# A fourth quarter of filters loaded earlier and rounded in two places, in a recommender's interaction layers

## The reference

```
e  = stack of the 32 picked rows              # 512 x 32 x 32: sample, field h, depth d
c0 = relu(sum over h,m of e[b,h,d]*e[b,m,d] *W0[h,m,n])    # 128 maps n
c1 = relu(sum over h,m of e[b,h,d]*c0[b,m,d]*W1[h,m,n])    # 128 maps n
z  = concat(sum_d c0, sum_d c1)               # 512 x 256
y  = relu(relu([z, dense] @ W1top + b1) @ W2top + b2) @ W3top
```

## Time and profile before

| | |
|---|---|
| median of 3 runs | 844.33 us (843.94 to 844.50) |
| the profiled execution's own time | 844.57 us |
| its span, first to last instruction | 842.8 us |
| PE busy | 833.8 us, 99% |
| DVE, ACT, POOL busy | 803.8, 782.7, 726.4 us |
| granted PE clock | full in every slice |
| DMA | 60.17 MB, mean 71 GB/s |

### The profile page before, as it was taken

One profiled execution on the slowest core, in us unless ns is written; L12 is line 12 of the kernel. 1 busy time (PEld: TensorE's weight loads), 2 busy tenths in 40 slices (PEclk: granted clock), 3 DMA queues, 4 the chain that ended last, 5 costly groups with the idle time before them and its releaser, 6 DMA issues.

```text
span 842.8 us, 17221 instructions
## 1 busy us (share of the span) xinstructions
PE 833.8 (99%) x3595; PEld 670.1 (80%) x3595; DVE 803.8 (95%) x877; ACT 782.7 (93%) x2779; POOL 726.4 (86%) x550
## 2 busy tenths in 40 slices
PE   8999999999999999999999999999999999999998
PEld 6687888888888888888888888888888888888777
DVE  7689999999999999999999999999999999999996
ACT  4799999999999999999999999999999999999984
POOL 5798888999888999888899888899888799988871
PEclk9999999999999999999999999999999999999999
DMA  4551233331232332132232123332123233112000
GB/s 147 166 155 40 56 83 81 83 84 51 43 85 78 82 85 67 29 82 78 83 84 78 30 69 79 83 83 84 41 53 82 79 84 84 47 48 76 1 13 1
DMA packets 62245, 60.17 MB, mean 71 GB/s; under 512 B 26347, under 2 KB 37227, under 8 KB 62222
## 3 DMA queue, kind: packets, MB, share of 16 engines
q1 hardware_dynamic: 58126, 57.80, 23.2%
q0 software_dynamic: 4096, 2.11, 3.3%
HBM read 55.51 MB, written 4.31 MB: 71 GB/s over the span
## 4 chain that ended last, share of the span: by engine, by line
PE 94%; DVE 2%; DMA 1%; POOL 1%; issue 1%; SPq 0%; ACT 0%; DVEq 0%
PE ps_y L895 27%; PE ps_y L903 27%; PE ps_y L896 27%; PE ps_c L868 3%; PE ps_c L878 3%; PE ps_c L877 2%; PE ps_c L876 2%; POOL gat L447 1%; DVE csum L737 1%; PE ps_c L874 1%; DVE prod L724 1%; DMA prod<-w 1%; DMA gat<-table,rows 0%; PE ps_y L999 0%; POOL w_lo L454 0%
## 5 line engine op out<-in xcount | busy, mean ns | idle before, releaser
L559 ACT ACTIVATE prod<-ps_y,es 128x128 f32<-128x128 f32 x2560 | 719.6, 490 | 37.3 <-PE ps_y L903 33.2
L737 DVE TENSOR_REDUCE csum<-prod 128x64 f32<-128x1664 f32 (+2 forms) x256 | 478.8, 1871 | 0.4 <-POOL prod L436 0.2
L895 PE MATMUL ps_y<-w_hi,c_both 128*128 128x512 f32 x1024 | 415.4, 406 | 2.9 <-POOL w_lo L454 2.1
L903 PE MATMUL ps_y<-w_hi,c_both 128*128 128x512 f32 x1024 | 399.6, 390 | 0.0
L896 PE MATMUL ps_y<-w_lo,c_both 128*128 128x512 f32 x1024 | 399.4, 390 | 0.0
L724 DVE TENSOR_TENSOR prod<-ps_y,es 128x512 f32<-128x512 f32 x384 | 256.3, 681 | 23.3 <-PE ps_y L903 17.0
L436 POOL TENSOR_TENSOR prod<-prod 128x768 f32<-128x768 f32 (+1 forms) x128 | 240.4, 1878 | 36.1 <-ACT prod L559 28.1
L895 PEld LDWEIGHTS ps_y<-w_hi,c_both 128*128 128x128 f32 x1024 | 192.4, 188 | 55.3 <-issue 11.5
L896 PEld LDWEIGHTS ps_y<-w_lo,c_both 128*128 128x128 f32 x1024 | 192.4, 188 | 48.2 <-issue 8.2
L903 PEld LDWEIGHTS ps_y<-w_hi,c_both 128*128 128x128 f32 x1024 | 192.2, 188 | 41.9
L426 POOL TENSOR_TENSOR z<-first,second 128x512 f32<-128x512 f32 x155 | 198.1, 1296 | 25.0 <-PE ps_c L874 24.9
(11 more groups left out here) (119 smaller groups left out, 290.0 us busy)
## 6 DMA issues: line engine op xcount, KB each, us to landing
second<-et_scratch SPq DMA_DIRECT2D x155, 256.0 KB, 3.6
first<-et_scratch SPq DMA_DIRECT2D x31, 256.0 KB, 3.3
et_scratch<-gat SPq DMA_DIRECT2D x62, 64.0 KB
prod<-w SPq DMA_DIRECT2D x4, 512.0 KB
h_scratch<-h_sums SPq DMA_DIRECT2D x120, 2.0 KB
gat<-table,rows_now POOLq DMA_INDIRECT x116
wt_sb<-wt SPq DMA_DIRECT2D x2, 512.0 KB
rows_now<-rows SPq DMA_DIRECT2D x30, 2.0 KB, 1.8
```

The costliest lines, as they stand in the source:

```text
L559: last = nc.scalar.activation(prod[:, buffer_of(g, u), h // 2, :, h % 2], ps_y[:, bank_of(g, u, k), j * N:(j + 1) * N], ACT.Copy, scale=es ...
L737: nc.vector.tensor_reduce(csum[:, g.r, maps, u], prod[:, buffer_of(g, u), fields_folded(g, u) // 2:F // 2, maps, :].rearrange("p a n t -> ...
L895: nc.tensor.matmul(out, hi, w_hi, start=True, stop=False)
L903: nc.tensor.matmul(out, lo, w_hi, start=False, stop=True).then_inc(y_ready, 1)
```

## The change

Two things are moved. In SP's order, the last quarter of W1 is issued directly behind the second and third, before the wait for group 1's gathers, and no more after group 1's two writes. In ACT's first tile, bank 6 of W1 is rounded ahead of bank 1's scaling, followed by the wait for the other tiles' products and their `round_z` (both stood ahead of bank 3); bank 7 alone is rounded ahead of bank 3. No instruction is added or removed.

```diff
             sp.wait_ge(gathered[0], 16 * TG)
-            for n in range(1, W1_LOADS - 1):
+            for n in range(1, W1_LOADS):
                 filters(n)
...
             send(Group(0, 1))
-            filters(W1_LOADS - 1)
             fetch(Group(0, 1))
...
-                        if number == 0 and (u, k) == (0, 3):
+                        if number == 0 and (u, k) == (0, 1):
+                            round_w1((6,))
                             act.wait_ge(z_ready, KP)
                             round_z(slice(1, TG), z_hi_ready, SPLIT)
-                            round_w1((6, 7))
+                        if number == 0 and (u, k) == (0, 3):
+                            round_w1((7,))
```

## The result

The changed kernel is slower: median 846.80 us of 21 runs (845.00 to 848.16), beside 844.30 us of 21 runs of the kernel before (843.71 to 846.41). The ratio is 1.0024, with a 95% interval of 1.0018 to 1.0029, so some 2.0 us were lost where 1.7 were to be won. (The ratio takes in every run of both and lies near that of the means, 846.70 and 844.59; the medians alone are 2.5 us apart. The profiled execution took 846.53 us, with a span of 844.7 us (842.8 before). Lines of the changed kernel are shifted by one here and there: L453 is the POOL split that was L454, L762 the DVE rest that was L761, L694 `rest_z` (L693), L932 the last first-layer matmul (L931), L567 ACT's rounding (L568).

A forecast was written before the change was run, and what follows sets the result against it. PE bounds the kernel, busy 833.8 of 842.8 us. The 2.55 us stall, less 0.21 for POOL's splits behind its gathers and 0.6 for DVE's hold, gives a gain of 1.7: 842.6 us, range 841.7 to 843.3.

The forecast's parts named there:

- What bounds the kernel, and that a gain is carried to the end: PE, full from 27 to 800 us, carries an earlier start through; the start's stall is worth 2.55 us at most.
- The transfer and ACT: Last W1 quarter landed by 18.3, bank 6 rounded from 19.6; nothing on ACT comes to the path, 0.5 us to spare.
- (c): Quarters in flight share the DMA engines, so the second lands with the last: slower, 845.0 to 845.6 us; chance 0.05.
- (d): Last quarter lands behind 19.6, ACT's order blocks, or group 1's rows come late: 843.0 to 844.3 us; chance 0.07.
- SP's queue: Group 1's gathers up to 1.3 us later, read-back from 20.4 to 21.7, POOL's products 0.4 to 1.7 earlier; cost none.
- POOL's two splits: Behind POOL's last gather, they would run from 21.62 to 24.15 without a hold, a gain of 2.34 us.
- That DVE can hold POOL: A POOL instruction starting under a DVE one with two SBUF operands may be held until it is through.
- The price of the hold: At POOL's splits beside DVE's L761 and L693: none, or POOL waits for both; -0.6 us in the sum.
- rival (b): POOL gets in between DVE's two instructions, rest_z is held, PE loses 1.21 us: gain 1.3, time 843.0; chance 0.17.
- The forecast's own case: POOL's first split waits for both DVE instructions, the second ends at 24.84: gain 1.7 us, time 842.6; chance 0.35.
- 0.21 + 0.6: Deductions from the 2.55 us stall: 0.21 for POOL's two splits behind its gathers, 0.6 for the hold by DVE.

The follow-up runs named there:

- e8: Changed kernel with DVE doing the rests of banks 6 and 7, POOL none, and ACT's order as before: 842.07 us beside 844.28, ratio 0.9975.
- e4: Changed kernel with ACT's order as in the kernel before, so only SP's earlier transfer remains: 843.44 us beside 844.47, ratio 0.9983.
- e2: Changed kernel with POOL's two last filter splits waiting until DVE's bank-5 rest is done: 843.52 us beside 844.47, ratio 0.9984.
- e7: Changed kernel with POOL's last gather behind its splits, the first split waiting for DVE's scaling of bank 2: 843.13 us, a single run.
- e9: Changed kernel with a one-column memset on POOL between last gather and first split, and a wait for it: 843.04 us beside 844.42, ratio 0.9980.
- e3: Changed kernel with 11 more matmuls of zeros filling PE's wait for rest_z: 845.35 us beside 844.47, ratio 1.0004.

## Why the prediction was wrong

**What bounds the kernel, and that a gain is carried to the end:** right. PE stayed full between 50 and 800 us, and e8 carried the 2.55 us of the start to the end: 2.8 us of the span, 2.1 by the ratio (1.4 to 2.9).

**The transfer and ACT:** right. The last quarter was issued at 11.7 and took 6.1 us, so it landed at 17.8 ("by 18.3"); bank 6 was rounded at 19.69 (19.6 predicted), `round_z` ended at 20.84 (20.9 predicted), the second quarter came no later (ACT idle 0.56 us before 15.15, against 0.67): rivals (c) and (d) didn't happen.

**SP's queue:** group 1's writes went out at 18.09, 1.0 us later than before, inside the 1.3 allowed. The read-back started at 21.98, not at 20.4 to 21.7: the writes took 2.6 us after their issue, not 2.0. POOL's first product started at 26.79, 0.17 us later than before, where 0.4 to 1.7 earlier was predicted. It cost nothing: no wait of PE follows from it.

**POOL's two splits:** in the changed kernel they weren't held at all: 21.80 to 24.31, where 21.62 to 24.15 was predicted without a hold and an end at 24.84 in the forecast.

**That DVE can hold POOL:** right, and the row it was read from, the gather at 10.98, is borne out by the other profiles. In each of the fourteen, one gather starts under a DVE rest of the filters, and it is longer than 0.94 us by what that one DVE instruction still has to run, less 0.12 or 0.13 us. In e8:

```profile
9.57 0.68 DVE L754 TENSOR_TENSOR w_lo<-prod,w_hi 128x512 fp32r<-128x512 f32 x1
9.73 1.35 POOL L446 DMA_INDIRECT gat<-table,rows  x1 [0.30 <-issue]
```

0.52 us were left, and the gather took 0.40 more. In e4 0.63 were left and it took 0.50 more; in the kernel before 0.40 and 0.28. The splits of e2, e4, e7 and e9 follow the same sum: in e9 0.49 were left of `rest_z`, and the split took 0.37 more. The gather at 20.66, which spoke against it, had started before the DVE rest, not under it. The forecast let POOL wait until both DVE instructions are through; the rows show a wait for the one that runs, after which POOL's split goes ahead of the next (e7). With POOL starting as late as in e4 and e9 that one is `rest_z`, the last of the two, so the size came out by this coincidence.

**The price of the hold is the step that failed.** The mechanism was named and its ends were worked out, but for the wrong party. "Its price from both ends" ran from nothing to POOL's split waiting for DVE, and rival (b) let DVE wait for one split, from the end of the bank-5 rest: 1.21 us. The worst end, DVE waiting for both splits and from the start of the bank-5 rest on, was left out: 2.81 us. What excluded it was the assumption that an instruction already running keeps its place. e2, e4, e7 and e9 show that this holds when POOL's instruction is released after it; in the changed kernel POOL's was released at 20.34, when ACT had rounded bank 6, behind a gather that ran until 21.70. The forecast's own case is e9 and e4, with POOL's second split ending at 24.79 in e9 (24.84 predicted), and their ratios are worth 1.7 and 1.4 us, the gain that was forecast. The Trainium skill's rule (SBUF — State Buffer, on its two separate sides and on who interferes with whom: whoever starts first gets the shared pair for the whole instruction) agrees with e2, e4, e7 and e9, by the lengths above; in the changed kernel it fails if it is read by the starts in the trace, since DVE's instruction stands at 21.23 and POOL's at 21.80.

**The clock had no term in the sum.** The earlier trace rows had it at 1.00 and PE's 1.74 us of idle time hadn't lowered it, and no rival carried a price for it. With 2.58 us it fell, for 1.55 us more. Without it the change would have been level with the kernel before, as far as can be told (e3).

In the sum, 2.81 us stand where 0.21 + 0.6 stood, 2.0 more; the clock and the restart, 1.65, had no term. 2.0 + 1.65 = 3.65 us is the distance between the gain of 1.7 and the 1.9 lost in the profiled span.

**Still open:** what in POOL lets a released instruction keep DVE out before the trace shows it start; and why with the halves DVE's rest got in when the gather was over, while with whole splits it did not until the last was through. The runs show the halves twice and the whole splits three times, and not the reason. In the changed kernel the trace has nothing of the split in POOL's queue before 21.70, when the gather is over. Nor does a run of its own tell the release apart from the moment of the start (e9).

## What to carry to other kernels

Before a tensor operation of POOL is moved, list the DVE instructions with two SBUF operands in its new place, and price both orders, with the whole row of POOL's instructions as the longest hold; one engine doing the work of both (here 1.2 us more on DVE) can be the better buy. A wait is also a spacer: the removed wait for a transfer had kept two engines apart, and a wait put back in the right place, even for a memset, was worth 3.7 us. For a new wait of PE as long as this one (2.6 us), add the price of a halved clock behind it (here 1.55 us).

## What was unexpected of the hardware

- A DVE subtraction of 128x512 with both operands in SBUF took 3.63 to 3.65 us instead of 0.68 in three profiles, whenever two POOL subtractions stood released behind a running gather; 2.41 with one; 1.22 with halves; 0.68 or 0.69 in every profile where POOL's was released later, stood behind no gather, or was left out.
- Released late, the two take turns: the one that runs finishes (POOL's first split 1.54 to 1.65 us instead of 1.28, longer by what the DVE instruction had left, less 0.12), and the one that has waited goes next (e7).
- The issue of a gather was stretched in the same way, from 0.94 us to 1.01 to 1.45, wherever it started under such a DVE subtraction, and not where the subtraction started under it.
- PE's clock fell to half after it had stood for 2.58 and 2.55 us (two profiles), was full again 4.4 and 3.0 us after PE had started again, and stayed full after 1.74, 1.3 and 0.7 us.
